# Sorting the edges of a graph network once, in message order, with edge matrices built over pairs of a group and a third of the sources

## The reference

```
edge_index = stack([src, dst])
x = ln(x + L0(x))   # alpha = x@wc ; beta = x@wn ; segment mean of beta[dst] over src ; + bias
x = ln(x + L1(x))   # 2 graph transformer layers: softmax over the edges into a node,
                    # 8 heads, then two batch norms and a feed-forward part
x = ln(x + L2(x))   # weighted graph convolution: weights edge_weight, normed by degree
x = ln(x + L3(x))   # msg = relu(x[src] + edge_attr@W_edge + b) ; aggr = segment_sum(msg, dst)
                    # then dense layers with layer norms and gelu
```

## Time and profile before

| what | before |
|---|---|
| median of 3 runs | 3059.01 us (3057.54 to 3060.01) |
| span of the profiled execution | 2795.5 us |
| own time of the profiled execution | not recorded apart; the runs lie within 2.5 us |
| median less span | 263.5 us |
| PE, DVE, ACT, POOL busy, share of the span | 90%, 76%, 60%, 46% |
| `sort_edges` | 0 to 302 us |
| `edge_matrices` | 302 to 614.5 us |
| `layer0` | 614.8 to 739 us |
| `layer1` | 739 to about 1750 us |
| `edge_messages` | 1916 to 2480 us |

### The profile page before, as it was taken

One profiled execution on the slowest core, in us unless ns is written; L12 is line 12 of the kernel. 1 busy time (PEld: TensorE's weight loads), 2 busy tenths in 40 slices (PEclk: granted clock), 3 DMA queues, 4 the chain that ended last, 5 costly groups with the idle time before them and its releaser, 6 DMA issues. The chain is left out here.

```text
span 2795.5 us, 45377 instructions
## 1 busy us (share of the span) xinstructions
PE 2528.3 (90%) x13039; PEld 1993.9 (71%) x13039; DVE 2138.1 (76%) x4172; ACT 1682.1 (60%) x3746; POOL 1299.1 (46%) x1279
## 2 busy tenths in 40 slices
PE   6999899999799999879899989598999999987887
PEld 4598555554488999648799984366888888765766
DVE  9699899998537888553588874866999999866667
ACT  1299888872226777413477761324888888845560
POOL 1777000007305677640377667315777777710211
PEclk9999999999899999998999999899999999988999
DMA  2210000013344453324455447225888888840201
GB/s 90 78 40 3 13 0 0 0 43 123 124 179 121 145 147 112 124 76 158 112 149 140 146 107 91 98 89 188 276 276 278 274 273 278 232 104 32 78 1 45
DMA packets 126768, 338.46 MB, mean 121 GB/s; under 512 B 25255, under 2 KB 39530, under 8 KB 126638
## 3 DMA queue, kind: packets, MB, share of 16 engines
q0 software_dynamic: 60768, 172.88, 22.0%
q1 hardware_dynamic: 65870, 163.93, 18.0%
HBM read 243.04 MB, written 85.82 MB: 118 GB/s over the span
## 5 line engine op out<-in xcount | busy, mean ns | idle before, releaser
L1839 POOL DMA_INDIRECT x_got<-table_dram,src_idx x376 | 418.8, 1114 | 117.3 <-issue 99.3
L722 POOL DMA_INDIRECT feature_rows<-in_edge_attr,ids x376 | 367.4, 977 | 117.4 <-issue 110.1
L1969 DVE TENSOR_TENSOR msg<-bank,x_got 128x512 f32<-128x512 f32 x376 | 252.7, 683 | 73.6 <-PE bank L1864 53.5
L1278 DVE TENSOR_TENSOR pt_low<-bank,pt_high 128x640 fp32r<-128x640 f32 x320 | 262.8, 822 | 54.9 <-ACT pt_high L1241 53.4
L673 ACT ACTIVATE hot_rest<-hot_dst,slot_w 128x128 bf16<-128x128 bf16 x864 | 272.6, 399 | 38.4 <-DVE hot_dst L633 38.4
L1241 ACT CAST pt_high<-bank 128x640 fp32r<-128x640 f32 x320 | 219.9, 688 | 117.6 <-PE bank L1192 117.4
L725 POOL COPY ids<-id_idx 128x136 uint32<-128x136 uint32 (+2 forms) x5 | 1.2, 242 | 612.5 <-DVE id_idx L840 347.6
L1918 ACT ACTIVATE msg_high<-msg 128x512 fp32r<-128x512 f32 x329 | 206.8, 628 | 74.8 <-DVE msg L1969 74.8
L1272 DVE CUSTOM_DVE_ANT_0 p<-bank,log_counts 128x1254 f32<-128x1254 f32 x160 | 232.6, 1454 | 13.7 <-PE bank L1175 13.6
L1192 PE MATMUL bank<-ident,p 128*128 128x128 f32 x1600 | 229.1, 275 | 2.3 <-DVE pt_low L1278 2.3
L1949 DVE SCALAR_TENSOR_TENSOR msg_low<-msg,msg_high 128x512 fp32r<-128x512 f32 x329 | 223.7, 680 | 0.0
(11 more groups left out here) (408 smaller groups left out, 6687.9 us busy)
## 6 DMA issues: line engine op xcount, KB each, us to landing
features_dram<-feature_parts POOLq DMA_DIRECT2D x94, 512.0 KB, 3.0
edge_got<-features_dram SPq DMA_DIRECT2D x94, 512.0 KB, 4.9
qk_dram<-qk_high SPq DMA_DIRECT2D x16, 640.0 KB, 2.9
qk_dram<-qk_low SPq DMA_DIRECT2D x16, 640.0 KB, 4.2
keys<-qk_dram SPq DMA_DIRECT2D x32, 320.0 KB, 4.7
queries<-qk_dram SPq DMA_DIRECT2D x32, 320.0 KB, 6.7
queries_low<-qk_dram SPq DMA_DIRECT2D x32, 320.0 KB, 8.9
acc_a<-zeros SPq DMA_DIRECT2D x1, 6400.0 KB, 30.6
```

Source lines behind the costliest of these rows:

```text
L722: pool.indirect_dma_start(out=rows[:, g % 2, j * ED:(j + 1) * ED], out_offset=None, in_=self.a.edge_attr_128, in_offset=bass.IndirectOffse ...
L1278: dve.tensor_tensor(p_low[:, made % 3, :, columns], unit(2 * n + u).rearrange("p (j n) -> p j n", n=P), p_high[:, made % 3, :, columns].bi ...
L1839: pool.indirect_dma_start(out=xg[:, g % XRING, j, :], out_offset=None, in_=k.table_dram, in_offset=bass.IndirectOffsetOnAxis(ap=k.src_idx[ ...
L1969: dve.tensor_tensor(msg[:, j, :], k.bank[:, 2 + j, :], xg[:, r, j, :], ALU.add).then_inc(added_x, 1)
```

## The change

- Edges are sorted by the same 30 buckets, but laid out at once in the order of the messages: only a block of `dst` begins a new group, and the three thirds of a block follow one another without padding. There are NG = 88 groups and NT = 352 tiles, in place of 108 and 432 for placing and 94 and 376 for messages.
- The moves of the tiles (L438 to L448 in part, L456 to L470, L561, L567, L605, L609) are gone. ACT copies the three fields out of the merged slots.
- A group can now hold sources of two or three thirds. `edge_matrices` runs over NPAIR = NG + 2 NB = 108 pairs of a group and a third. A table `pairs` of 3 rows by 108, made on one partition by DVE, holds for each pair its place in the accumulators, the third's first column and the group's first tile. Pairs that are not used point at four empty tiles behind the last (NTX = 356).
- In `build`, DVE reads the first tile and the first column of the pair from the table with two `value_load`s. `hot_src` is compared over the columns `col` to `col + 417` of the row of node numbers (`col` is 0, 417 or 834) and no longer over its first 417. ACT reads the first tile with one `value_load`. `add` keeps its own.
- The accumulators are cleared by ACT (9 pieces of 512), POOL (6) and DVE (4) in place of ACT (15) and DVE (5).
- ATTEND_GROUPS is 32 in place of 34, LAYER_GROUPS 40 in place of 42, FIRST_GROUPS 8 in place of 10.
- The loop of `edge_messages` on DVE has four groups ahead of it and 21 turns of four, in place of two and 23.

The core of the diff:

```diff
-NG = -(-((E + NK3 * (P - 1)) // P + NB * (GT - 1)) // (2 * GT)) * 2
-NG3 = -(-(E // GE + NK3) // 2) * 2
-NT, NT3 = NG * GT, NG3 * GT
+NG = (E + NB * (GE - 1)) // GE
+NT = NG * GT
+NPAIR = NG + 2 * NB
+NTX = NT + GT
...
-            me.then(dve.tensor_copy(tiles_i[:, 0, :], in_tiles[:]))
...
-            for c in range(TC):
-                dve.tensor_scalar(moves[:, c, :], k.node_row[0:TP, 1:NT + 1], new_tile[0:TP, c:c + 1], None, ALU.is_equal).then_inc(moves_made, 1)
...
-            for q, part in enumerate(MOVED):
-                pe.wait_ge(merged, q + 1)
-                for c in range(TC):
-                    t = pe.transpose(ps_d[0:TP, q, c * P:(c + 1) * P], slots[:, c * TP:(c + 1) * TP, part], k.ident[:])
-                t.then_inc(slots_turned, 1)
...
@@ edge_matrices, on DVE
             def build(g, u):
+                tile0 = dve.value_load(k.pairs[0:1, 2, bass.ds(g, 1)], min_val=0, max_val=NT)
+                col = dve.value_load(k.pairs[0:1, 1, bass.ds(g, 1)], min_val=0, max_val=2 * C3)
 
                 def of_tiles(values):
-                    return values[:, bass.ds(g * GT, GT)].unsqueeze(1).to_broadcast([P, P, GT])
+                    return values[:, bass.ds(tile0, GT)].unsqueeze(1).to_broadcast([P, P, GT])
...
-                    last = dve.tensor_scalar(hot_src[:, u, j, 0:C3], k.node_row[:, 0:C3], k.slot3_src[:, bass.ds(t, 1)], None, ALU.is_equal)
+                    last = dve.tensor_scalar(hot_src[:, u, j, 0:C3], k.node_row[:, bass.ds(col, C3)], k.slot3_src[:, bass.ds(tile0 + j, 1)], None, ALU.is_equal)
...
             def add(g, u):
-                to = dve.value_load(k.place3[0:1, bass.ds(g, 1)], min_val=0, max_val=(NB - 1) * NP + 2 * C3)
+                to = dve.value_load(k.pairs[0:1, 0, bass.ds(g, 1)], min_val=0, max_val=(NB - 1) * NP + 2 * C3)
...
@@ edge_matrices, on ACT
                     act.wait_ge(chunk_done, g * 2 + 2)
+                    tile0 = act.value_load(k.pairs[0:1, 2, bass.ds(g, 1)], min_val=0, max_val=NT)
                     act.wait_ge(hots_built, g * 2 + 1)
...
-LAYER_GROUPS = 42
-ATTEND_GROUPS = 34
+LAYER_GROUPS = 40
+ATTEND_GROUPS = 32
```

More of the change, by code:

```diff
@@ L287, in _ @@
             sp.wait_ge(alpha_added, NB)
-            for acc, first, end in ((acc_c, ACC_BY_ACT, NB * NP // 512), (acc_a, 0, NB * NP // 512)):
+            for acc, first, end in ((acc_c, CLEARED, NB * NP // 512), (acc_a, 0, NB * NP // 512)):
                 sp.dma_start(acc[:, first:end, :], zeros[:].unsqueeze(1).to_broadcast([P, end - first, 512])).then_inc(zeroed, 16)
@@ L413, in _ @@
                 column(c)
[L415 to L418, removed]
+            start = by_block(AHEAD)[:, :, 0]
+            key, div, col, group = (key_f[:, j, :] for j in range(4))
+            me.mark(dve.tensor_tensor(span_f[:, 0, :].rearrange("p (b t) -> p b t", t=3), by_block(AHEAD), of_block(start), ALU.subtract))
@@ new lines, in _ @@
+            me.then(dve.scalar_tensor_tensor(span_f[:, 1, :].rearrange("p (b t) -> p b t", t=3), by_block(THROUGH), float(GE - 1), of_block(start), ALU.add, ALU.subtract))
+            me.then(dve.tensor_copy(span_i[:], span_f[:]))
+            me.then(dve.tensor_scalar(small_i[:], span_i[:], GE.bit_length() - 1, None, ALU.arith_shift_right))
+            me.then(dve.tensor_copy(span_f[:], small_i[:]))
+            me.then(dve.tensor_tensor(row(FROM), span_f[:, 1, :], span_f[:, 0, :], ALU.subtract))
@@ new lines, in _ @@
+            me.then(dve.tensor_tensor(reached[:], k.groups_row[0:1, :].unsqueeze(2).to_broadcast([1, NPAIR, NK3]),
+                                      row(PAIRS)[0:1, :].unsqueeze(1).to_broadcast([1, NPAIR, NK3]), ALU.is_ge))
+            me.then(dve.tensor_reduce(key, reached[:], axis=AX, op=ALU.add))
+            me.then(dve.tensor_tensor(reached[:], reached[:], span_f[0:1, 0, :].unsqueeze(1).to_broadcast([1, NPAIR, NK3]), ALU.mult))
+            me.then(dve.tensor_reduce(group, reached[:], axis=AX, op=ALU.add))
@@ L419, in _ @@
+            me.then(dve.tensor_tensor(group, group, k.groups_row[0:1, :], ALU.add))
+            me.mark(dve.tensor_scalar(k.pairs[:, 2, :], group, float(NG), float(GT), ALU.min, ALU.mult))
+            me.then(dve.tensor_scalar(key, key, -1.0, None, ALU.add))
             me.then(dve.tensor_scalar(div, key, 171.0, None, ALU.mult))
@@ L453, in _ @@
             me.then(dve.tensor_copy(k.blk[:], k.blk_f[:]))
[L456 to L462, removed]
-            for c in range(TC):
[L464 to L468, removed]
-            for c in range(TC):
-                dve.tensor_scalar(moves[:, c, :], k.node_row[0:TP, 1:NT + 1], new_tile[0:TP, c:c + 1], None, ALU.is_equal).then_inc(moves_made, 1)
+            me.mark(dve.memset(k.slot3_src[:, NT:NTX], 0.0))
+            me.mark(dve.memset(k.slot3_dst[:, NT:NTX], 0.0))
+            me.mark(dve.memset(k.slot_w0[:, NT:NTX], 0.0))
             for c in range(SHOTS, PE_COLS):
@@ L596, in _ @@
             act.copy(pe_w[:], ps_p[:, 3, :]).then_inc(high_copied, 1)
[L598 to L609 removed]
+            for i in range(CLEARED - BY_DVE_LAST - BY_POOL):
+                act.activation(acc_c[:, i, :], k.node_row[:, 0:512], ACT.Copy, scale=0.0)
+            for q, (part, to) in enumerate(zip(MOVED, (k.src_idx, k.slot_dst, k.id_idx))):
+                act.wait_ge(merged, q + 1)
+                act.copy(to[:], slots[:, :, part])
 def edge_matrices(nc, k):
```

172 lines of the change are left out of this document (77 added, 95 removed).

## The result

The changed kernel took 3106.2 us (median of 4 runs, 3104.81 to 3115.38), the kernel before 3059.5: the ratio is 1.0159, 95% interval 1.0143 to 1.0174, 47 us slower. The prediction said 3110.

A forecast was written before the change was run, and what follows sets the result against it. PE was taken as full in edge_matrices, with DVE within 4%, and in edge_messages; ACT and PE in sort_edges. 97 - 33.8 - 9.7 - 0.3 - 2.5 = +50.7; 2795.5 + 50.7 + 263.5 = 3109.7, say 3110 us; own range 3090 to 3138, whole 3062 to 3142.

The forecast's parts named there:

- The 263.5 us "kept as the difference": Whole kernel: medians stand 263.5 us above the profile's span of 2795.5 us; kept as a constant and added to the sum.
- edge_matrices, two loads: DVE in edge_matrices: two added loads stretch acc_c to hot_dst from 1.01 to 1.75 us, +97 us in all.
- the turn of the loop: edge_matrices: end-of-turn arithmetic, before hidden by acc_a, costs 0.3 us every second group, 0.15 per group.
- the 3 us for the ends: edge_matrices: +3 us for the loads of the first and last builds, outside the loop's 106 turns.
- the lower bound of the load: edge_matrices: a load holds the sequencer only 0.305 us and 0.1 of arithmetic, +0.28 per group, +30 us.
- The shifted window: hot_src in edge_matrices, odd first column: taken as nothing, bound +35 us; rival that it costs a mode, chance 0.08.
- PE's clock: edge_matrices: stays 1.00; rival that it falls from 2.4 to 1.2 GHz, +303 us, 3316 us, chance 0.05.
- edge_messages: edge_messages: 24 tiles fewer at 1.408 us per tile with PE full, -33.8 us.
- attend: Both attend stages: next stage waits for POOL alone; two feature groups fewer free 6.9 + 2.8 us, -9.7 us.
- sort_edges: sort_edges: only the shorter DVE chain behind the merge gains, 11.1 to about 8.7 us: -2.5 us (+1 to -5).
- The merge waits for the slots read back: sort_edges: merge at 290.59 waits for slots from DRAM, behind POOL's unchanged scatters, so earlier columns gain nothing.
- 8 us of hidden gain: sort_edges: small operations shrink from 12.4 to about 4 us, columns restart 8 us earlier, hidden by the merge's wait.

The follow-up runs named there:

- b_again: The kernel before, unchanged, profiled once more (the second profile): 3057.09 us, span 3055.3.
- a_cols272: The changed kernel with PE placing 272 columns in place of 160 (PE_COLS): 3072.0 us.
- b_cols272: The kernel before with PE placing 272 columns in place of 160, nothing else: 3037.0 us, ratio 0.9926.
- a_cols320: The changed kernel with PE placing all 320 columns and POOL scattering none: 3093.3 us (one run).
- b_two_loads: The kernel before with two register loads, values unused, added at the head of build in edge_matrices: 3142.8 us, ratio 1.0281.
- a_skip: The changed kernel with the bounds check left out behind DVE's three register loads per pair: 3041.6 us, ratio 0.9946 to the kernel before.

## Why the prediction was right, and where it was not

**The number.** +50.7 us was forecast, +47 measured. That it came so close is in part luck: the total hides errors that cancel, in the order of the table -11.8, +8.3, +0.6, +7.2, 0, -9.9 and +2.2, together -3.4.

**The 263.5 us "kept as the difference".** This step failed as such: they are no constant around the span, but delays inside `sort_edges` (169), `edge_messages` (76) and `layer1` (17), the second profile less the first. It did no harm to the total because the changed kernel has delays of nearly the same size, for which the prediction gave no reason. Those of `sort_edges` hang on POOL's 160 scatters, which the change keeps: `a_cols272`, `b_cols272` and `a_cols320` show it. What the others hang on no run shows. It did harm to three terms that I read from stages without their usual delays: `sort_edges`, `attend` and `edge_messages`.

**edge_matrices, two loads.** The mechanism was right, and the step almost to the hundredth: 1.75 us forecast, 1.74 measured, with starts of two loads 0.71 us apart as I took them. Under-sized was the turn of the loop: 0.3 estimated, 0.53 measured (2.27 against 1.74), which makes 0.11 per pair, 12 us. In `a_cols272` the same turn costs 0.28, so my 0.3 fits the programs with the quick branch and misses the changed kernel. Two smaller errors made the forecast too large, by 3 us each: the 3 us for the ends did not come, and the new period was set against 2.81 us, the sum of DVE's two steps, though my own count gave 2.84 for the old period. The lower edge of 3090 in the forecast's own range follows from no bound either: the lower bound of the load, +30 us, gives 3043.

By the Trainium skill's page "DMA: Bandwidth & Descriptors", section "Latency and other measured facts", a `tensor_load` takes some 600 ns at least. Here, in `b_two_loads`, 0.62 us lie between the starts of two loads, 0.305 of them the record and most of the rest the bounds check, and without the check (`a_skip`) the next instruction follows 0.34 after the load's start. So the floor fits the load with its check, not the load itself.

**The shifted window.** Nothing, as taken: 319 to 331 ns for all 432, where before they took 321 to 331. The 4-byte condition of the Trainium skill's page "VectorE: DVE Perf Modes", section "Mode 2×_1P", does not show here; that rival is out.

**PE's clock** stayed at 1.00 in `edge_matrices` with PE 79% busy: that rival is out too. It did fall to 0.50, but in the rows of `sort_edges` above, where PE was 17% and 21% busy.

**edge_messages.** The count of 24 tiles was right, the pace came from the wrong execution: 62 gathers per 100 us are 1.61 us per tile, 38.7 us. Of the other 5 us, 2 to 3 are how executions differ, and the rest I cannot name: the stage takes 638 to 643 us in the five profiles of a kernel with 376 tiles (the first one left out), and 597 to 603 in the seven with 352, 41 us less on average.

**attend.** The failed step is "the next stage starts after POOL's sequencer alone". In the usual executions DVE's last work ends 18 and 13 us later, counted from the start of each stage, and POOL waits 22 and 19 us behind its own last work, where in the first profile the 7.84 were its sequencer's. So compute ends last, and two groups fewer free nothing.

**sort_edges.** "The merge waits for the slots read back" failed for the same reason: POOL is done at 281 us and PE at 444, so the columns are the end of the chain, and what lets them start earlier counts in full. They end 13.4 us earlier in the changed kernel (PE's last placing matmul starts at 444.2, against 457.6). In the second profile of before PE has nine columns done when it goes on at 302.9, behind the small operations that follow `alpha`; in the changed kernel it has 17 done, between the pauses, at 297.9. From there both take 1.025 us per column. Those small operations, which I had put at 8 us of hidden gain, run from 289.85 to 301.51 before, with nothing but the nine columns beside them. How much of the 13 us they give was not tried apart.

## What to carry to other kernels

- A register load is work of the sequencer, and its price is what the engine's instructions ahead of it do not cover. In a loop where DVE was 96% busy the first added load cost 0.23 us a group and the second 0.53. Pack what a turn needs into one word, leave out the check where the table is clamped by construction, and then look at the turn of the loop itself.
- Where a profile fitted its times here, its span was some 2 us short (1.8 in `b_again`, 1.9 in the changed kernel). If they differ by much more, profile once more before any term is read from it. A rival of the form "the profiled execution is not the usual one" belonged in the prediction.
- When two engines share a task (160 columns each here), find the division by experiment: PE had placed 16 of its 160 columns (none in the kernel before) when POOL's scatters were over, so the halves ran nearly one after the other.

## What the runs showed of the hardware

- While POOL issued indirect scatters one every 1.3 us, PE fell behind in two ways. It issued straight-line matmuls 2.1 to 2.8 us apart, waiting for nothing that the profile shows, at the lower clock level once it had begun; and DVE and ACT went on some 18 us or more behind PE's last record. It did not begin with the first scatter: in `b_again` scatters start at 66 us and PE keeps its full pace until 102. It ended within 19 us of the last scatter in the changed kernel, before, and with 272 columns, and was absent without scatters. One execution of before, with the same 160 scatters, did not have it. What is waited for stays open, and so does why that execution was spared; whether the slower pace in `edge_messages` and `attend`, where POOL gathers, is the same effect was not tried.
- One load of three registers: 746 ns, of one: 305.
- The same loop on the sequencer took 0.23 us more or less per turn in programs that differ only ahead of it, 0.12 of them between the branch and the next instruction.
